# Softmax reciprocal of an attention stage spread over 64 partitions through DRAM instead of by a matmul

## The reference, cut to what matters

```python
xn = layernorm(x)
q = xn @ q_w.T + q_b
xd = conv1d(xn, conv_w, stride=2, depthwise) + conv_b     # 2048 -> 1024 rows
k, v = xd @ k_w.T + k_b, xd @ v_w.T + v_b
att = softmax(einsum('bhnd,bhmd->bhnm', q, k) / 8)
attn = merge_heads(einsum('bhnm,bhmd->bhnd', att, v)) @ out_w.T + out_b
h = gelu(einsum('th,ehi->tei', xn, W1) + b1)              # 4 experts, 1024 -> 4096
ffn = layernorm(sum_e onehot(argmax(xn @ W_router))[:, e] * h[:, e] @ Wo + bo + xn)
out = x + attn + ffn
```

## Time and profile before

| | us |
|---|---|
| median of 8 runs | 4713.08 |
| range of the 8 runs | 4700.7 to 5303.87 |
| the profiled execution, device time | 4701.11 |
| its span on the slowest core (core 4) | 4699.5 |
| shortest span of a core | 4669.9 |
| PE busy (matmuls) | 3778.2 (80%) |
| DVE busy | 2037.1 (43%) |
| ACT busy | 1574.1 (33%) |

### The profile page before, as it was taken

One profiled execution on the slowest core, in us unless ns is written; L12 is line 12 of the kernel. 1 busy time (PEld: TensorE's weight loads), 2 busy tenths in 40 slices (PEclk: granted clock), 3 DMA queues, 4 the chain that ended last, 5 costly groups with the idle time before them and its releaser, 6 DMA issues.

```text
span 4699.5 us, 53924 instructions; the slowest of 8 cores (4669.9 to 4699.5 us)
## 1 busy us (share of the span) xinstructions
PE 3778.2 (80%) x15040; PEld 1493.7 (32%) x15040; DVE 2037.1 (43%) x3620; ACT 1574.1 (33%) x2245; POOL 110.7 (2%) x213
## 2 busy tenths in 40 slices
PE   4579999598878888889535799995988888888883
PEld 3331222143333333333233312221333333333331
DVE  3504577233255255155345144773332552552544
ACT  4223466133133133133033234662331331331330
POOL 1001111000000000000000000000000000000000
PEclk9985799699999999999755866997999999999996
DMA  6225666223543533543311100001235435344432
GB/s 141 59 36 111 122 120 124 62 113 138 112 138 145 112 146 136 112 161 126 72 68 37 36 18 1 1 1 54 108 144 112 162 121 141 132 163 107 152 117 67
DMA packets 98372, 473.49 MB, mean 101 GB/s; under 512 B 10976, under 2 KB 11008, under 8 KB 56112
## 3 DMA queue, kind: packets, MB, share of 16 engines
q1 hardware_dynamic: 68896, 352.38, 20.3%
q0 software_dynamic: 29200, 117.66, 15.0%
HBM read 537.15 MB, written 50.33 MB: 125 GB/s over the span
## 4 chain that ended last, share of the span: by engine, by line
PE 66%; DMA 19%; DVE 6%; issue 5%; ACT 3%; SPq 0%; DVEq 0%; ACTq 0%; POOL 0%; POOLq 0%
PE ps L997 30%; DMA w1r<-scrW 10%; PE psOT L626 7%; PE psS L718 7%; PE ps L1061 6%; DMA wor<-wo 5%; PE psBC L649 3%; PE psOT L679 3%; PE psC L516 2%; PE psA_r L392 2%; PE psA_tr L366 2%; PE psC L562 1%; DMA rowsl<-rows 1%; PE psC L538 1%; DMA arena<-x 1%
## 5 line engine op out<-in xcount | busy, mean ns | idle before, releaser
L997 PE MATMUL ps<-xnT,w1r 128*128 128x512 bf16 x8192 | 1847.0, 385 | 247.0 <-DMA w1r<-scrW 198.0
L997 PEld LDWEIGHTS ps<-xnT,w1r 128*128 128x128 bf16 x8192 | 794.6, 99 | 1296.5 <-issue 405.8
L1006 ACT ACTIVATE gbuf<-ps,b_sb 128x512 bf16<-128x512 f32 x1024 | 701.6, 687 | 1367.1 <-PE ps L997 1105.9
L727 ACT ACTIVATE etb<-psS 128x1024 bf16<-128x1024 f32 x512 | 523.2, 1024 | 395.5 <-PE psS L718 378.2
L1061 PE MATMUL ps<-wor,interT 128*128 128x512 bf16 x2048 | 466.1, 389 | 72.7 <-DMA wor<-wo 64.6
L1015 DVE TENSOR_TENSOR sel<-gbuf,mbc 128x512 bf16<-128x512 bf16 x256 | 108.9, 425 | 846.9 <-ACT gbuf L1006 846.9
L626 PE MATMUL psOT<-etb,v 128*65 128x512 bf16 x1024 | 376.0, 455 | 0.0
L718 PE MATMUL psS<-qT,kT 64*128 64x512 bf16 x1024 | 366.5, 444 | 4.0 <-DVE v L572 2.0
L1061 PEld LDWEIGHTS ps<-wor,interT 128*128 128x128 bf16 x2048 | 201.0, 100 | 337.8 <-issue 117.2
L639 DVE RECIPROCAL arena<-psOT 1x512 f32<-1x512 f32 x64 | 214.5, 3352 | 213.6 <-PE psOT L626 213.4
L366 PE MATMUL psA_tr<-eye_f,arena 128*128 128x128 f32 x256 | 90.5, 444 | 249.0 <-DVE arena L346 114.8
(11 more groups left out here) (102 smaller groups left out, 2544.8 us busy)
## 6 DMA issues: line engine op xcount, KB each, us to landing
w1r<-scrW SPq DMA_DIRECT2D x256, 1024.0 KB, 7.5
wor<-wo POOLq DMA_DIRECT2D x64, 1024.0 KB, 8.5
castslot<-w POOLq DMA_DIRECT2D x128, 256.0 KB, 4.9
scrW<-castslot SPq DMA_DIRECT2D x128, 256.0 KB, 3.1
arena<-x SPq DMA_DIRECT2D x16, 1024.0 KB, 7.0
arena<-x SPq DMA_DIRECT2D x32, 512.0 KB, 5.4
out<-arena SPq DMA_DIRECT2D x32, 512.0 KB, 2.9
wslot<-qwT POOLq DMA_DIRECT2D x2, 2048.0 KB, 14.3
```

Source lines behind the costliest of these rows:

```text
L727: E.emit("scalar", lambda s, par_=spar, pair_=pair, eo=eoff: s.activation(etb_t[:, eo + pair_ * 1024:eo + (pair_ + 1) * 1024], ps_s[par_][ ...
L997: t_.matmul(ps8[:, gp_ * 512:(gp_ + 1) * 512], w1r[:, sl_, cc_ * 512 + ic_ * 128:cc_ * 512 + (ic_ + 1) * 128], xnT[:, cc_, 8 + tb_ * 512:8 ...
L1006: E.emit("scalar", lambda s, e_=e, icg_=icg, gp_=gpar: s.activation(gbuf[:, icg_ % 2, e_, :], ps8[:, gp_ * 512:(gp_ + 1) * 512], AF.Gelu, ...
```

## The change

The ones matmul, its PSUM bank and the copy are gone. Instead SP stores the reciprocal row of 512 floats to a small DRAM tensor `sgd` (two rows, used in turn), waits for that store, and loads the row back into all 64 partitions of `rcbc`; the multiplication on DVE waits for this load. The bank that is free becomes a fourth slot of the `psOT` ring.

```diff
-        NOT = 3
+        NOT = 4
...
-              nc.psum_tensor(f"psBC{b}", [128, 512], F32) as ps_bc):
+              nc.psum_tensor(f"psOT3{b}", [128, 512], F32) as ps_ot3):
...
                     rrows[sl_], ring[r_][64:65, :]),
-                    waits=[(sT, m_ot[(pqb, ph_)]), (sT, m_bcpar[sl])], incs=[(sV, 1)])
+                    waits=[(sT, m_ot[(pqb, ph_)]), (sSG[sl], m_sgstore[sl])],
+                    incs=[(sV, 1)])
...
-                E.emit("tensor", lambda t_, sl_=sl: t_.matmul(
-                    ps_bc[0:64, :], ones_f[0:1, 0:64], rrows[sl_],
-                    start=True, stop=True),
-                    waits=[(sV, m_recip[(pqb, ph_)]), (sV, m_rcbc)], incs=[(sT, 1)])
-                mbc = sT.n
-                m_bcpar[sl] = mbc
-                E.emit("vector", lambda v: v.tensor_copy(rcbc, ps_bc[0:64, :]),
-                       waits=[(sT, mbc), (sV, m_rcbc)], incs=[(sV, 1)])
-                mrcp = sV.n
+                E.emit("sync", lambda s, sl_=sl: s.dma_start(
+                    sgd[sl_:sl_ + 1, :], rrows[sl_]),
+                    waits=[(sV, m_recip[(pqb, ph_)]), (sSG2[sl], m_sgload[sl])],
+                    incs=[(sSG[sl], 16)])
+                m_sgstore[sl] = sSG[sl].n
+                E.emit("sync", lambda s, sl_=sl: s.dma_start(
+                    rcbc, sgd[sl_:sl_ + 1, :].broadcast_to((64, 512))),
+                    waits=[(sSG[sl], m_sgstore[sl]), (sV, m_rcbc)],
+                    incs=[(sSG2[sl], 16)])
+                m_sgload[sl] = sSG2[sl].n
                 E.emit("vector", lambda v, a=hp2, b2=hh2, r_=pr: v.tensor_tensor(
                     otp[64 * b2:64 * (b2 + 1), a, :], ring[r_][0:64, :], rcbc,
                     op=ALU.mult),
-                    waits=[(sV, mrcp), (sT, m_otp_free)], incs=[(sV, 1)])
+                    waits=[(sSG2[sl], m_sgload[sl]), (sT, m_otp_free)], incs=[(sV, 1)])
```

More of the change, by code:

```diff
@@ L117, in build_nc @@
     eye_d = nc.dram_tensor("eye", [128, 128], F32, kind="ExternalInput").ap()
+    sgd = nc.dram_tensor("sgd", [2, 512], F32, kind="Internal").ap()
     st = contextlib.ExitStack()
@@ L129, in build_nc @@
     sCSTO = [mksem(f"sCSTO{i}") for i in range(2)]
+    sSG = [mksem(f"sSG{i}") for i in range(2)]
+    sSG2 = [mksem(f"sSG2{i}") for i in range(2)]
     sSCR = [mksem(f"sSCR{i}") for i in range(2)]
@@ L593, in phaseC @@
               nc.psum_tensor(f"psOT2{b}", [128, 512], F32) as ps_ot2,
-              nc.psum_tensor(f"psBC{b}", [128, 512], F32) as ps_bc):
+              nc.psum_tensor(f"psOT3{b}", [128, 512], F32) as ps_ot3):
             ps_s = [ps_s0, ps_s1]
-            ring = [ps_ot0, ps_ot1, ps_ot2]
-            m_ring = [None, None, None]
+            ring = [ps_ot0, ps_ot1, ps_ot2, ps_ot3]
+            m_ring = [None, None, None, None]
             rslot = [0]
@@ L633, in phaseC @@
             m_recip = {}
-            m_bcpar = [0, 0]
+            m_sgstore = [0, 0]
+            m_sgload = [0, 0]
             def sigma_recip(pend):
```

## The result

The changed kernel is slower: it takes 1.0213 times the time of the kernel before, interval 1.0189 to 1.0236, and the middle of its runs is 4809.06 us (4789.75 to 4826.47). Some executions of every kernel here, before as after, have one group of cores at a lower clock and take longer; all ratios and this middle leave them out, while the plain median after, 4966 us, does not. The profiled execution after took 4818.4 us, its span 4816.8 (core 5).

The account below looks back on a forecast made before the run. PE was taken to bound the attention. Batch 0's loss of 155 us behind the weight pieces less batch 1's gain of 76 adds 79 to 4701.1, 4780; allowing for the median, 4786 us, range 4735 to 4855.

Parts of the forecast that it names:

- PE bounds the attention, and batch 1 gains: Both batches' attention: PE is busy throughout and sets the pace; batch 1, where SP is idle, gains 76 us.
- 45.0 + 2.6: Batch 1's later three blocks: 45 ones matmuls of 1.00 us gone, plus copy and gap before three output projections.
- L: Time from the end of a reciprocal on DVE to the landing of its row's load, taken as 4.3 us.
- DVE's pace: Batch 1 at 2.4 GHz: two heads take at least 4.03 + L, so 4.17 us a head, under PE's 4.33.
- by a hair: Batch 1 at 2.4 GHz: ACT's 4.28 us a head hides just under PE's 4.33.
- Batch 0 goes at the pieces' pace: Batch 0: reciprocal stores queue on SP behind three weight pieces a head, 12.9 us; batch 0 loses 155 us (140 to 210).
- the 44 us from the pieces' end to the attention's end: Batch 0 before the change: weight pieces were read as ending 44 us before the attention, at 866.1 us.
- 1 us at every second block of SP: Batch 0: SP stands between row store and load, delaying ready weight-piece stores 15 times in 31 heads; 15 us.
- the 99th: Batch 0: last weight piece ahead of head 31's reciprocal store on SP, loaded at 803.97 us; second projection begins at 814.2.
- The pieces got slower, not faster: Batch 0 rival: SP's block spreads the buffers, a weight piece takes 3.45 us instead of 4.295, kernel 4681; chance 4%.
- The clock of batch 1's first block: Rival: without the float32 matmul this block gets 2.4 GHz, gaining 52 us more, kernel 4728 or 4734; chance 8%.
- A long L: Rival: 6.5 us from reciprocal to landed load, late blocks of both batches at 5.27 a head, kernel 4879 or 4885; chance 15%.

## Why the prediction was right, and what was mis-sized

**PE bounds the attention, and batch 1 gains: right.** From first to last projection of batch 1 it gained 46.1 us on the cores' mean, forecast 45.0 + 2.6; the first block 28.8 against 28.4, the whole of batch 1 74.9 against 76. L is 4.20 us at the median where 4.3 was taken, so DVE's pace is (4.03 + 4.20) / 2 = 4.1, under PE's 4.33 as forecast; only on core 5, with 4.5 to 4.7, is it level. What is level with PE everywhere is ACT: the forecast read 4.28 us for four exponentials, which leaves out the pause between two heads' exponentials, and back to back they take 4.32 to 4.34. So "by a hair" was no margin at all, and the whole gain came out because the two are equal. The Trainium skill, "DMA: Bandwidth & Descriptors", section on the anatomy of one DMA, gives about 2.0 us as the fixed cost of a DMA issued from GpSimd. Here, on SP, the row's store needed 1.28 to the issue of the load, and the load 2.8 from issue to landing (medians), so twice that figure fits the pair's sum, 4.1, and the figure neither of its parts.

**Batch 0 goes at the pieces' pace: right.** The waits and their order are those of the forecast; a head takes 14.1 us on the cores' mean instead of 12.9, since the pieces got slower. The first projection was put at about 610 and came at 617.7 on the cores' mean. From the second projection to the attention's end it took 1023.9 + 15.7 - 845.1 = 194.5, forecast 191.5. One reading was loose, without effect on the sum: the 44 us from the pieces' end to the attention's end count from the last load; its store lands at 829.5, so it is 37.

**The mis-sized term is what the pair does to the pieces.** It was taken as 1 us at every second block of SP, 15 us up to the second projection, in bounds of 0 to 70. Measured on the cores' mean, a piece takes 0.335 us more, and the 99th is loaded at 831.9 instead of 802.2, 30 us later. The step that failed is the one that priced only SP's standing. That standing is worth what its removal gave back, 845.1 - 828.8 = 16 us with the row store on ACT, close to the 15. But it is made up otherwise, of some 0.5 us at each of 31 heads and not of 1 us at every second, so the agreement is in part luck. The other half, the pair's traffic beside the pieces, was not in the sum: 15 us. A further 3 lie between the 99th load and the second projection (13.2 us, forecast 10.2), where L was taken from a quiet queue: beside the pieces it is 2.3 from store to load and 3.7 more to the landing. These 18 us, 3 more after the second projection and 1 less gain in batch 1 make 22; the middle of the runs, 4809, lies 23 over the forecast.

**The rivals.** The pieces got slower, not faster. The clock of batch 1's first block stayed at 0.50, so the float32 matmul was not what held it there. A long L came where pieces run beside the pair (6.4 us in the run with the stores on POOL), but not at 2.4 GHz in batch 1, where it would have cost.

## What to carry to other kernels

A DMA pair put on a queue that waits for other transfers makes its consumer run at the pace of those transfers; read the program order of that queue before the price of the pair. The same change can gain in one phase and lose in another: price it by phase, and keep it only where it gains. Whether a queue's order is the cause can be tried by changing how much stands ahead of the new instruction.

## What the runs showed of the hardware that was not expected

The granted clock of an attention block can be lost within the block. In the run with the stores on POOL (core 0), at 2.4 GHz, one wait of 1.49 us of PE was followed by a fall from 1.00 to 0.50 within 4 us, and 60 us of PE busy 60 of 60 did not bring it back; the next output projection did. The Trainium skill, "TensorE: Matmul & The Clock Gate", section on a second failure mode, describes a PE with short idle gaps that swings between the two clocks; here the fall agrees, and there was no swing back within the block.

A pair stores 2 KB and writes 128 KB, half of what one piece loads, and yet its traffic alone cost the pieces beside it about 0.5 us a pair, in two kernels that issue it in different ways (0.47 and 0.52; 0.4 to 0.7 where it ran beside the first block alone).
